# First loads begun by SyncE, output squares by chunk, query-key product behind the gating, gated values turned in steps three and five

## What is computed

```python
x = x + 0.5 * ffn(layernorm(x))      # x: 4 x 512 tokens, 512 wide
x = x + attn(layernorm(x))
x = x + 0.5 * ffn(layernorm(x))

def ffn(h):                          # 512 -> 2048 -> 512
    gate_w, up_w, down_w = spline_reconstruct(...)   # Catmull-Rom over few control points
    return (silu(h @ gate_w.T) * (h @ up_w.T)) @ down_w.T

def attn(x):                         # 16 key heads, 32 value heads of 128
    q, k, v, z = split(x @ W_qkvz); b, a = split(x @ W_ba)
    q, k, v = silu(causal_conv4(q, k, v))
    q, k = rms(q) / 128, rms(k) / 128 ** 0.5
    beta, g = sigmoid(b), -exp(A_log) * softplus(a + dt_bias)
    for t in tokens:                 # state S: 128 x 128 for each value head
        S = S * exp(g[t]); delta = (v[t] - k[t] @ S) * beta[t]
        S = S + outer(k[t], delta);  o[t] = q[t] @ S
    return (silu(z) * rms(o) * norm_w) @ W_out
```

## Time and profile before

| | us |
|---|---|
| median of 3 runs (lowest, highest) | 3639.86 (3639.62, 3641.59) |
| the profiled execution, its own time | 3643.73 |
| its span, first to last instruction | 3641.8 |
| PE busy | 3397.8 (93%) |
| ACT, POOL, DVE busy | 2090.7, 2268.9, 2282.5 (57%, 62%, 63%) |

### The profile page before, as it was taken

How to read it: one execution, slowest core, us unless ns; L and a number is a source line. 1 busy time by engine, 2 the same in 40 slices (tenths; PEclk the granted TensorE clock), 3 DMA queues, 4 the chain that set the end, 5 groups by cost and what they waited for, 6 DMA issues and landing times. The chain is left out here.

```text
span 3641.8 us, 77463 instructions
## 1 busy us (share of the span) xinstructions
PE 3397.8 (93%) x29092; PEld 2448.0 (67%) x29092; DVE 2282.5 (63%) x4402; ACT 2090.7 (57%) x5699; POOL 2268.9 (62%) x2680
## 2 busy tenths in 40 slices
PE   5799599999999999999999999999999999995998
PEld 3587266666666666666666666666666666663787
DVE  4464566666666666666666666666666666663564
ACT  2334466666666666666666666666666666662343
POOL 2011477777777777777777777777777777772010
PEclk8899799999999999999999999999999999998999
DMA  3342411212121212121212122222222222112321
GB/s 140 140 78 28 87 62 60 85 60 85 60 85 60 85 60 85 60 85 60 85 60 90 62 85 70 83 73 76 78 77 71 76 77 68 60 59 73 135 55 35
DMA packets 217314, 274.47 MB, mean 75 GB/s; under 512 B 91248, under 2 KB 127344, under 8 KB 215792
## 3 DMA queue, kind: packets, MB, share of 16 engines
q1 hardware_dynamic: 205008, 251.37, 22.5%
q0 software_dynamic: 4464, 14.36, 1.1%
q10 hardware_dynamic: 7472, 3.79, 0.5%
HBM read 180.12 MB, written 89.16 MB: 74 GB/s over the span
## 5 line engine op out<-in xcount | busy, mean ns | idle before, releaser
L2095 ACT ACTIVATE at_t<-at_inv 128x512 f16<-128x512 f32 x768 | 460.8, 600 | 434.5 <-PE at_inv L1903 434.3
L2332 DVE TENSOR_TENSOR at_pml<-at_prod,at_cst 128x256 f16<-128x256 f32 x768 | 323.1, 421 | 212.6 <-PE at_prod L1677 201.1
L2479 POOL TENSOR_TENSOR at_gm<-at_cst,at_gates 128x512 fp32r<-128x512 f32 x256 | 268.2, 1069 | 230.4 <-PE at_misc L1677 230.4
L1677 PE MATMUL at_proj<-x_hi,at_w_hi 128*128 128x512 f16 x1024 | 390.2, 381 | 2.6 <-PEq L1263 2.6
L1677 PE MATMUL at_proj<-x_lo,at_w_hi 128*128 128x512 f16 x1024 | 390.8, 382 | 0.0
L1677 PE MATMUL at_proj<-x_hi,at_w_lo 128*128 128x512 f16 x1024 | 390.1, 381 | 0.0
L1901 PEld LDWEIGHTS at_inv<-at_pml,at_t 128*128 128x128 f16 x3072 | 226.4, 98 | 119.1 <-DVE at_pml L2332 81.1
L1677 PE MATMUL at_prod<-at_t,at_nlhi 128*128 128x64 f16 (+1 forms) x3584 | 287.5, 197 | 19.1 <-DVE at_cv_z L2374 15.6
L2205 DVE SCALAR_TENSOR_TENSOR at_cv_v<-at_proj,at_cw,at_cv_v 128x511 f32<-128x511 f32 (+2 forms) x384 | 287.5, 749 | 21.8 <-ACT at_cv_v L2019 8.3
L1901 PE MATMUL at_inv<-at_pml,at_t 128*128 128x64 f16 x3072 | 286.1, 194 | 11.8 <-DVE at_pml L2332 1.1
L2249 DVE SCALAR_TENSOR_TENSOR rows<-at_misc,first_tab,rows 128x512 f32<-128x512 f32 x256 | 191.1, 747 | 164.2 <-PE at_misc L1677 164.2
(11 more groups left out here) (323 smaller groups left out, 10140.6 us busy)
## 6 DMA issues: line engine op xcount, KB each, us to landing
rows<-x SPq DMA_DIRECT2D x64, 1024.0 KB, 5.6
x<-rows SPq DMA_DIRECT2D x64, 1024.0 KB, 4.3
at_gb<-decays SPq DMA_DIRECT2D x64, 512.0 KB, 3.7
at_raw_w<-w_qkvz SPq DMA_DIRECT2D x48, 512.0 KB, 7.3
ffn_weights<-ffn_w SPq DMA_DIRECT2D x1, 11776.0 KB, 37.6
ffn_w<-ffn_weights POOLq DMA_DIRECT2D x4, 2688.0 KB, 23.4
at_raw_o<-w_out SPq DMA_DIRECT2D x16, 512.0 KB, 3.6
f_xnext<-x_in SPq DMA_DIRECT2D x4, 1024.0 KB, 5.3
```

Source lines behind the costliest of these rows:

```text
L1677: return nc.tensor.matmul(out, lhsT, rhs, start=start, stop=stop)
L2095: own["a_t"].up(A(grown(t16[:, s % R].rearrange("p a t -> p (a t)"), s // R), grown(psT[s % R], s // R), ACT.Copy))
L2332: own["d_p"].up(V.tensor_tensor(pml[:, level - 1, g].rearrange("p (c b a m) -> p c b a m", c=CH, a=2, m=m)[:, :, :, 0, :], psP[:, 0:S // 2 ...
L2479: last = G.tensor_tensor(gm[:, k], incl.unsqueeze(1).to_broadcast([P, CH, P]), new_gates[:, g, at:at + CH, h:h + 1].to_broadcast([P, CH, P ...
```

## The change

- The seven first loads move from ACT's list to SP's, between the loads of tile 0 and the store of the spline weights. SP waits there for `first.cleared`.
- The squares are taken chunk by chunk: two in each of chunks 0 to 2 while the next chunk is computed, and only the last two behind the last chunk. PE now raises `s_o` for every chunk and waits for the squares of chunk `c - 1` before it writes the outputs of chunk `c`. The gating of each head waits for that head's last square.
- POOL's addition of a constant to the scale's sum (L2430) moves from the start of the slot to the end of the slot before.
- On DVE, the second convolution tap of the key moves ahead of the gating. Of the two query-key instructions the first moves directly behind the gating, at the end of the slot before, the second to step 2, and the third tap of the key moves from step 2 to step 3. The taps of the query start in step 5 instead of 6, the remainders go to steps 4 and 6, the last row addition from step 11 to 10.
- On PE, the turns of the gated values move from steps 4 and 6 to 3 and 5, and the gate products are dealt out anew (4, 6, 4, 6, 4 in steps 3 to 7, where there were 5, 5, 5, 2, 7).
- On ACT, the tap of the query moves from step 4 to 2, the tanh of the second value head from 2 to 4.

```diff
@@ ffn_phase, SP
+                def load_first():
+                    w_qkvz, w_out, w_ba_in, norm_w, bits_in = first_in
+                    for i in range(3):
+                        sp.dma_start(raw[i]...).then_inc(first.loaded, 16)
+                    sp.dma_start(raw[3]..., w_out[0:R * D, :]...).then_inc(first.loaded, 16)
...
+                    if t == 0 and first:
+                        load_first()
                     if t == 0 and w_known:
                         sp.dma_start(w_dram, wts[:].bitcast(F32)).then_inc(w_stored, 16)
@@ ffn_phase, ACT
-                if first:
-                    w_qkvz, w_out, w_ba_in, norm_w, bits_in = first_in
-                    for i in range(3):
-                        act.dma_start(raw[i]...).then_inc(first.loaded, 16)
...
@@ attn_phase, PE
-                    fill[3].append(gates_in(Z0_U, 0, 5))
-                    fill[4].append(gates_in(Z0_U, 5, 10))
-                    fill[5].append(gates_in(Z0_U, 10, 15))
-                if behind:
-                    for h in range(R):
-                        fill[4 + 2 * h].append(lambda h=h: turn_gated(h, j - 1))
-                if has_delta:
-                    fill[6].append(gates_in(Z0_U, 15, 17))
-                    fill[7].append(gates_in(Z0_U, 17, 24))
+                    fill[3].append(gates_in(Z0_U, 0, 4))
+                    fill[4].append(gates_in(Z0_U, 4, 10))
+                    fill[5].append(gates_in(Z0_U, 10, 14))
+                    fill[6].append(gates_in(Z0_U, 14, 20))
+                    fill[7].append(gates_in(Z0_U, 20, 24))
...
+                    for h in range(R):
+                        fill[3 + 2 * h].append(lambda h=h: turn_gated(h, j - 1))
...
                             wait(pe, "p_qg", R * j + R)
+                            wait(pe, "a_sqo", SQ * j + c)
...
-                        if c == CH - 1:
-                            own["s_o"].up(last)
-                        else:
+                        own["s_o"].up(last)
+                        if c < CH - 1:
                             turn_v(c + 1)
@@ ACT
-                def squares(h):
-                    wait(act, "s_o", j + 1)
-                    wait(act, "p_fr", j)
-                    if h < R - 1:
-                        wait(act, "d_gate", R * j + h + 1)
-                    for c in range(CH):
-                        last = A(osq[:, h, c * P:(c + 1) * P], ch(psO[h], c), ACT.Square, ...)
+                def squares(c, h):
+                    if c == 0:
+                        wait(act, "p_fr", j)
+                    wait(act, "s_o", CH * j + c + 1)
+                    return A(osq[:, h, c * P:(c + 1) * P], ch(psO[h], c), ACT.Square, ...)
...
+                    if has_delta and c < CH - 1:
+                        squares_of(c)
...
-                    for h in reversed(range(R)):
-                        squares(h)
+                    for h in range(R):
+                        own["a_sqo"].up(squares(CH - 1, h))
@@ DVE
+                if has_delta:
+                    steps[2].append(lambda: qk(j, 1))
                 if has_prep and has_delta:
-                    steps[2].append(lambda: conv(K_U, (3,)))
-                if has_delta:
-                    for h in range(R):
-                        steps[3].append(lambda h=h: qk(h))
+                    steps[3].append(lambda: conv(K_U, (3,)))
...
+                if has_prep and j + 2 < UNITS:
+                    conv(K_U, (2,), j + 1)
                 if has_delta:
                     for h in range(R):
-                        if h == 0:
-                            wait(dve, "s_o", j + 1)
-                        else:
-                            wait(dve, "a_sqo", R * j + h)
+                        wait(dve, "s_o", CH * (j + 1))
+                        wait(dve, "a_sqo", SQ * j + CH + h)
                         own["d_gate"].up(V.tensor_tensor(gated_of(h), psO[h]..., gated_of(h), ALU.mult))
-                if has_prep and j + 2 < UNITS:
-                    conv(K_U, (2,), j + 1)
+                if has_prep:
+                    qk(j + 1, 0)
@@ POOL
-                    chain(G.tensor_scalar(flat, flat, Q_EPS * EPS_RMS, None, ALU.add))
...
+                    wait(pool, "a_sq", j + 1)
+                    own["p_qe"].up(G.tensor_scalar(qe[:, nxt, :], qe[:, nxt, :], Q_EPS * EPS_RMS, None, ALU.add))
```

75 lines of the change are left out of this document (40 added, 35 removed).

## The result

| | before | after |
|---|---|---|
| median of 4 runs (lowest, highest), us | 3640.31 (3639.62, 3641.59) | 3673.92 (3672.44, 3676.24) |
| the profiled execution, its own time and span | 3643.73, 3641.8 | 3675.31, 3673.5 |
| PE busy | 3397.8 (93%) | 3367.0 (92%) |

The change makes the kernel slower: the ratio is 1.0093, 95% interval 1.0075 to 1.0110, or 33.6 us between the medians. The prediction was 3670 us.

A forecast was written before the change was run, and what follows sets the result against it. PE's list was taken to set the pace in the attention, with a stall behind ACT's load issue before it. From a median of 3639.9, loads -29 and slots +59 gave 3670 us; 8-in-10 range 3608 to 3698.

The forecast's parts named there:

- main case: Whole kernel: the loads gain and the attention slots lose more, 3670 us, own range 3650 to 3690; chance 0.76.
- loads -29: Ahead of the first silu: SP issuing the seven loads saves 28.1 us of stall and 2.0 of clock, less 1.0.
- slots +59: Attention: each slot grows by 0.94 us; 62 slots plus 0.7 for first and last make +59 us.
- PE goes on at 88.9 and not at 117.05: First cells: PE's stall until the first silu nearly vanishes, 28.1 us less.
- These 2.0 us: After the stall, 117.05 to 121.48: PE ran at half clock; without the long idle stretch 2.0 us are gained.
- small transfers of POOL: Cells 11 to 14: POOL's transfers may come late beside the store, +1 us, ends 0 and 4.
- the loads don't help: Rival, first cells: the stall belongs to the transfers, so only 5 us of issue time is saved; 3694 us, chance 0.07.
- The wait: Step 3: PE's first gate product waits for the key's last tap, now behind the masking; PE stands for 1.33 us.
- The 1.8 us from POOL are worth 0.43: First turn: POOL would allow it 1.8 us earlier, but the tap's wait leaves 6.47 against 6.90.
- only about 0.4 us of a slot could be won in the end: Faster rival, attention: all of POOL's 1.8 us reaches the output product; -25 us more, 3585, chance 0.05.
- +0.35 - 0.15: Step 11: row addition ahead of the masking delays it 0.35 us; the key's turn no longer waits about 0.15.
- The squares at nothing: Attention chunks: six squares moved into ACT's idle time there were costed at nothing.

The follow-up runs named there:

- the late store: The kernel before, loads still issued by ScalarE, with SyncE's 11776 KB store of the spline weights issued one tile later: 3637.30 us, ratio 0.9990.
- The kernel with the turns back: The changed kernel with turns, gate products, taps, remainders and last row addition in their old steps; loads and the slot's end stay changed: 3578.98 us, ratio 0.9824.
- the chain shortened: The changed kernel with tap and addition back, ACT's copies of turned values ahead of the corrections' copies, POOL's split behind the key's scale: 3524.79 us, ratio 0.9681.

## Why the prediction was right

**Size and sign.** 3670 us were forecast, 3673.92 measured, inside the main case's own range of 3650 to 3690. Both terms were 1 to 4 us too small: loads -29 against -30.4 (alone) and about -31 in the changed kernel; slots +59 against +63. They have opposite signs, so the errors cancel in part, which is luck; the mechanism behind each is not.

**The loads.** "PE goes on at 88.9 and not at 117.05": it doesn't stop at all. The sum let the table load start only with the gate product complete, at 87.0; it started right behind the copy, at 86.34, and the silu followed 1.36 us later, at 87.70. "These 2.0 us" of the clock came: share 1.00 through both windows. Gap and clock make 30.2, and the first tile ends 29.96 us earlier. The term of +1 for "small transfers of POOL" measured 0; its bounds of 0 to 4 were too narrow a picture of the risk, as the late store shows. Of the rest up to the attention's first `at_fr` 1.6 us lie in the normalising phase, from the last turn of the fourth tile (364.54 before, 334.58 after) to the attention's first product (434.21, 402.61): 69.67 us at a mean granted clock of 0.69 against 68.03 at 0.75, with the same busy times on the other engines. Why the clock differs there isn't known.

That "the loads don't help", which is how the Trainium skill has it in "DMA: Bandwidth & Descriptors", "Issuing engines are not separate DMA queues", is refuted here: ACT's seven issues took 29.9 us together (85.07 to 115.08), and PE stood for 28.19 us behind them. That issuing time is what was saved fits the section; that it is usually small does not hold in this case. What the section says of the transfers themselves (they run on the same DMA engines whoever starts them) does agree with the kernel that left three loads on ScalarE: they landed in 31.5 us beside the store.

**The wait.** In slot 31, for which it was worked out, the schedule was met within 0.05 us at each step: step 2 at 3.08 (3.05 forecast), gate products at 6.03 (6.03), first turn at 6.48 (6.47), second at 9.31 (9.26), output product at 12.08 (12.03). In the median of all slots this product came 0.87 us later than before and not 0.74, which is most of what the slots' term lacked. (The "about 1.3 us" of idle time named as a sign is 1.17 in the profile, which counts from the end of the product before.) Taking the tap back and moving it alone show that it is the cause.

**POOL.** "The 1.8 us from POOL are worth 0.43" holds only beside the wait. The kernel with the turns back shows what the earlier scale, with the rest of the slot's end, can give: 0.64 us up to the output product, 0.55 a slot. I had said that in that line "only about 0.4 us of a slot could be won in the end"; that was too low, and with the chain shortened the slot fell by 1.36 us. The figure was the weakest of the prediction, since it had no schedule behind it.

**The end of the inverse.** "+0.35 - 0.15" for the addition and the key's turn, so 0.20: the corrections of step 11 came 0.31 us later, the key's turn 0.14, and the part of the slot behind the first output product grew by 0.15. The slot lost 1.00 us in all, against 0.94.

**The squares at nothing.** Right in three of four slots: with them and without the wait the part of the slot behind the output product is as long as before (slots 0.66 shorter where the product is 0.64 earlier). In every fourth slot 0.4 us were lost again to the wait for `at_kn`; further along, this wait went when POOL's split was moved, and not the squares.

## What to carry to other kernels

An instruction that nothing delays should not be queued behind one that waits for another engine: one DVE tap, moved from ahead of a mask to behind it, cost 0.6 us in each slot of the old kernel and 1.3 in each of the new, more than all that the rest of the change gained there. When an engine is made early, ask what stands next in line before counting the gain, and price the pieces apart, since a bundle that measures +34 us here held parts worth -30 (loads), -34 (the slot's end) and +97 (the turns, the tap, the addition and what was dealt out anew with them). A large store should be put where no small transfer that someone waits for runs beside it, and loads that are wanted soon should be issued ahead of it, by an engine that has nothing else to do.

## What was not expected of the hardware

- One ScalarE issue took 24.94 us beside an 11776 KB store of SyncE, and 0.53 us without it. Three loads of 512 KB were still issued in 2.27 us ahead of it, beside the same store; this fourth one was held. With the store in eight pieces two issues were held, for 11.55 and 12.90 us.
- While the store was in flight its queue and ScalarE's passed the same number of packets, 176 of 47 KB and 175 of 1 KB in 90 to 110 us, and 738 and 736 with the store in pieces; GpSimd's 2 KB transfers beside the late store the same, 220 each in 186 to 210 us. A load of small packets beside a store of large ones so gets a small share of the bytes. The Trainium skill's "DMA: Bandwidth & Descriptors", "Queues, rings and completion order", says that each DMA engine takes packets from its queues in turn, and the traces agree. In 84 to 118 us as a whole SyncE's queue moved 12.18 MB in 349 packets and ScalarE's 2.13 MB in 2333, because ScalarE's passed freely once the store had drained.
- GpSimd's 2 KB transfers, 1.9 us to landing as a rule, took up to 27.8 us beside the late store (15.8 by the median of that stretch), and ACT waited 24.55 us for them.
